# A vision tower on one core: the feed-forward's output columns in three pieces of nearly equal width

## The chip, the core and the metric

One of the eight cores of a Trainium2 chip runs the whole program. The core has TensorE (PE, with its weight loads shown as PEld), VectorE (DVE), ScalarE (ACT), GpSimd (POOL) and SyncE (SP, which here only issues DMAs). The metric is the device time of one execution in microseconds, median of several runs.

## What is computed

The input has 64 x 128 positions of states; the output has 64 rows of 129 tokens of 1024 channels. Three stages follow each other: a state-space kernel that turns each position into 1024 channels, a bidirectional state-space block behind a layer norm (down to 128 channels, two rounds, up again, with a residual), and a feed-forward part behind another layer norm, with a residual. The change touches the feed-forward part alone:

```python
def _L0_ffn_ref(x, base_W, base_b, router_W, router_b, A, B, expert_map):
    SCALING = 32.0 / 16.0
    E = A.shape[0]                                                        # 8 experts of rank 16
    base_out = jnp.einsum('btd,od->bto', x, base_W) + base_b              # 1024 -> 1024
    logits = jnp.einsum('btd,nd->btn', x, router_W) + router_b            # 1024 -> 15
    probs = jax.nn.softmax(logits, axis=-1)
    topk_p, topk_i = jax.lax.top_k(probs, E)
    mapped = expert_map[topk_i]
    onehot = (mapped[..., None] == jnp.arange(E)).astype(x.dtype)
    w = jnp.einsum('btk,btke->bte', topk_p, onehot)
    h = jnp.einsum('btd,erd->bter', x, A)                                 # 1024 -> 8 * 16 = 128
    lora = jnp.einsum('bter,eor->bto', h * w[..., None], B) * SCALING     # 128 -> 1024
    return base_out + lora
...
h = h + _L0_ffn_ref(_layernorm(h, axis=-1), ...)
```

## The kernel before

The work is cut into 65 tiles of 128 tokens (64 pairs of rows and one tile for the class token). It is pipelined by hand over iterations: in iteration i the first stage works on tile i, the state-space block on tiles i-1 and i-2, the up-projection and the second layer norm on tile i-4 (td in the code) and the feed-forward part on tile i-5 (te). Each engine has a `body` in which its steps stand in a fixed order, written out by hand; nothing but these lists and semaphores sets the order. `Step` holds one semaphore for each kind of step; `per` says how many increments a tile makes, and `wait(eng, n, name=j)` waits until tile n has made j of them. Iterations 8 to 61 run in a hardware loop of two iterations a turn, the others are written out.

On TensorE a tile's feed-forward is one product with a contraction of 1024 (eight slices k of 128) against the columns of `w_hi` and `w_lo`: 1024 columns of base_W, 128 of lora_A, 15 of the router and one of zeros. Each slice takes three matmuls (`ffn`, L1545: high part by high weights, high by low weights, low by high weights). The columns go to three banks of PSUM: `bases(0, ..)` and `bases(1, ..)` write 512 columns each to bank 0 and bank 1, and `route(a, b)` writes the 144 columns of lora_A and the router to bank 2. The pieces of `bases` and `route` stand between the steps of the other stages in the list at the end of TensorE's body: all of `route` and half of `bases` between `turn_x` and `project_out`, the rest of `bases` between `project_out` and `lora`. A matmul of 128 x 512 with `row_sel` (L1563) adds the bias at the start of each base half.

VectorE reads the router's logits out of bank 2 (`router(0)`, L1330), ScalarE takes the exponential, VectorE goes on (`router(1)` to `router(8)`), and `router(8)` (L1352) writes HW, the 128 lora columns weighted by expert. TensorE turns HW (`turn_h`, L1569, into bank 2), ScalarE and VectorE split it into HWS (`keep_w`, `weighted_lo` L1313), and TensorE adds the lora product to banks 0 and 1 (`lora(0)`, `lora(1)`, L1575 to L1577, 512 columns each). VectorE then adds both banks to the residual in HB (`final(0)`, `final(1)`, L1452), and SyncE stores HB.

Names of other steps that the next parts speak of: `project_out` (L1749) ends the state-space block's product, `layer_out` (L1319) copies it to U, `gated_b` (L1393) makes GT; `project_bc` (L1669) and `up` (L1587 to L1590) on TensorE wait for GT or its split GTS; `residual(h)` (L1401) adds the up-projection's halves to HB; `stats_2` (L1408) is the second layer norm's statistics, `shift_2` (L1421) its mean, `split_lo` (L1428) the low part of the normalized tile.

## Time and profile before

| | |
|---|---|
| median of 3 runs | 2318.59 us (2317.51 to 2318.93) |
| span of the profiled execution | 2315.8 us |
| TensorE busy | 2160.1 us, 93% of the span, 14117 matmul instructions |
| VectorE busy | 1843.7 us, 80% |
| ScalarE busy | 1527.5 us, 66% |
| GpSimd busy | 1095.6 us, 47% |
| `ffn` matmuls (L1545), 512 columns | 3 x 1040 instructions |
| `ffn` matmuls (L1545), 144 columns | 3 x 520 instructions |

The profiled execution is one run; its span goes from the first to the last instruction. The first 250 us prepare weights, then the iterations run. Matmuls are pipelined: one begins before the last has ended, so the busy time of a matmul (its duration) is longer than its distance to the next start, and a busy TensorE is not one at its peak.

### The profile page before, as it was taken

How to read it: one execution, taken by the hardware profiler on the slowest of the kernel's cores; microseconds unless marked ns; L12 is line 12 of the kernel's file. 1: busy time of each engine (PE TensorE's matmuls, PEld its weight loads, DVE VectorE, ACT ScalarE, POOL GpSimd, SP SyncE). 2: the span in 40 equal slices, each digit the busy share in tenths (PEclk: the TensorE clock that was granted, in tenths of full speed). 3: DMA queues.
4: the chain of work that ended last, by engine and by line, in shares of the span. 5: the costliest groups of instructions: out<-in, count | busy, mean ns of one | idle time of the engine just before them, and what ended most of it. 6: DMA issues, size and time to landing. Idle time of an engine off the chain costs nothing.

```text
span 2315.8 us, 51899 instructions
## 1 busy us (share of the span) xinstructions
PE 2160.1 (93%) x14117; PEld 1805.7 (78%) x14117; DVE 1843.7 (80%) x4980; ACT 1527.5 (66%) x2921; POOL 1095.6 (47%) x1350
## 2 busy tenths in 40 slices
PE   2366999999999999999999999999999999999997
PEld 2245888888888888888888888888888888888776
DVE  8666788888888888888888888888888888887763
ACT  4465676667766677666777667676676766767552
POOL 5543554445544455444554445544455444554321
PEclk8577999999999999999999999999999999999999
DMA  5201111222112221122221222212222112221111
GB/s 150 65 26 36 56 51 47 64 64 64 50 46 64 64 64 58 37 64 64 64 61 35 64 64 64 63 34 61 64 64 64 35 60 64 64 64 38 62 40 34
DMA packets 90061, 132.61 MB, mean 57 GB/s; under 512 B 20379, under 2 KB 63559, under 8 KB 90006
## 3 DMA queue, kind: packets, MB, share of 16 engines
q1 hardware_dynamic: 87496, 126.12, 18.4%
q10 hardware_dynamic: 2510, 5.83, 0.8%
q8 instruction: 25, 0.41, 0.1%
q14 instruction: 30, 0.25, 0.0%
HBM read 55.17 MB, written 76.74 MB: 57 GB/s over the span
## 4 chain that ended last, share of the span: by engine, by line
issue 44%; PE 27%; POOL 9%; DVE 7%; ACT 6%; POOLq 1%; DVEq 0%; ACTq 0%
PE bank L1644 5%; PE bank L1545 5%; POOL CB L934 4%; PE bank L1600 3%; PE bank L1575 2%; DVE NF L1274 2%; ACT L1039 2%; POOL XD L885 2%; PE bank L1718 2%; PE bank L1702 2%; POOL RS L919 1%; PE bank L1577 1%; PE bank L1576 1%; POOL RS L898 1%; PE bank L1692 1%
## 5 line engine op out<-in xcount | busy, mean ns | idle before, releaser
L1545 PE MATMUL bank<-w_hi,XHI 128*128 128x512 f32 (+1 forms) x1560 | 623.0, 399 | 0.0
L1545 PE MATMUL bank<-w_lo,XHI 128*128 128x512 f32 (+1 forms) x1560 | 555.1, 356 | 0.0
L1545 PE MATMUL bank<-w_hi,XLO 128*128 128x512 f32 (+1 forms) x1560 | 554.6, 355 | 0.0
L1180 DVE SCALAR_TENSOR_TENSOR CX<-bank,cw,CX 128x252 f32<-128x252 f32 (+5 forms) x804 | 335.6, 459 | 62.2 <-ACT CX L977 62.0
L934 POOL TENSOR_TENSOR CB<-CB,CM 48x252 f32<-48x252 f32 (+5 forms) x402 | 293.1, 729 | 153.5 <-ACT CM L962 142.6
L1545 PEld LDWEIGHTS bank<-w_hi,XLO 128*128 128x128 f32 x1560 | 295.5, 189 | 46.9
L1545 PEld LDWEIGHTS bank<-w_lo,XHI 128*128 128x128 f32 x1560 | 297.0, 190 | 41.2
L1545 PEld LDWEIGHTS bank<-w_hi,XHI 128*128 128x128 f32 x1560 | 296.7, 190 | 41.2
L962 ACT ACTIVATE T<-bank 64x512 f32<-64x512 f32 x256 | 151.4, 591 | 261.9 <-PE bank L1634 257.2
L898 POOL TENSOR_TENSOR RS<-VE,half_neg 128x1 f32<-128x1 f32 x65 | 35.5, 546 | 370.7 <-DVE VE L1372 370.7
L925 POOL TENSOR_TENSOR RB<-m_gt,AS 128x512 fp32r<-128x512 f32 x134 | 165.0, 1231 | 56.9 <-DVE AS L1446 56.9
L962 ACT ACTIVATE CM<-CR,cwb 48x256 f32<-48x256 f32 x402 | 181.4, 497 | 3.7 <-POOL CB L934 1.5
L892 POOL TENSOR_TENSOR RS<-MS,half_neg 128x2 f32<-128x2 f32 x67 | 46.9, 700 | 244.2 <-DVE MS L1303 244.2
L1634 PE MATMUL bank<-VB,W 128*128 128x256 f32 x512 | 149.4, 416 | 7.8 <-DVE W L1245 5.8
L1428 DVE TENSOR_TENSOR XLO<-bank,XHI 128x512 fp32r<-128x512 f32 x130 | 89.9, 692 | 73.1 <-ACT XHI L962 73.1
L1434 DVE TENSOR_TENSOR RF<-m_lt,AS 128x512 fp32r<-128x512 f32 x134 | 142.8, 1104 | 0.0
L962 ACT ACTIVATE XHI<-bank 128x512 fp32r<-128x512 f32 x130 | 77.6, 597 | 95.3 <-PE bank L1600 95.3
L1644 PE MATMUL bank<-XHT,wdT 128*128 128x128 f32 x1040 | 135.4, 286 | 4.5 <-ACT XHT L962 4.5
L1644 PEld LDWEIGHTS bank<-XHT,wdT 128*128 128x128 f32 x1040 | 129.2, 202 | 6.1 <-ACT XHT L962 6.1
L877 POOL TENSOR_TENSOR NB<-GB,sp_dt 128x512 f32<-128x512 f32 x67 | 96.0, 1433 | 77.5 <-DVE GB L1257 77.5
L885 POOL TENSOR_TENSOR XD<-XS,DD 128x512 f32<-128x512 f32 x67 | 84.7, 1264 | 98.5 <-DVE DD L1265 53.2
L1292 DVE TENSOR_TENSOR XD<-bank,XD 128x512 f32<-128x512 f32 x67 | 46.4, 692 | 79.1 <-POOL XD L885 58.2
(295 smaller groups left out, 5375.1 us busy)
## 6 DMA issues: line engine op xcount, KB each, us to landing
carried<-T SPq DMA_DIRECT2D x65, 512.0 KB, 4.7
T<-carried SPq DMA_DIRECT2D x65, 512.0 KB, 3.8
out<-HB SPq DMA_DIRECT2D x129, 256.0 KB, 3.2
tables<-tab SPq DMA_DIRECT2D x8, 560.0 KB, 4.1
TB<-tables SPq DMA_DIRECT2D x64, 70.0 KB, 2.7
carried<-U SPq DMA_DIRECT2D x65, 64.0 KB, 3.5
XM<-carried SPq DMA_DIRECT2D x65, 64.0 KB, 4.7
XI<-in_x SPq DMA_DIRECT2D x128, 32.0 KB, 2.7
```

Source lines behind the costliest of these rows:

```text
L877: inc(pool.tensor_tensor(NB[:, :, :].rearrange("p (a h) t -> p a h t", a=2), GB[:, :, :].unsqueeze(2).broadcast_to([P, 2, NH, CS]), dtB, A ...
L885: inc(pool.tensor_tensor(XD[:, :, :], v3(XS[:, :], HD), DD[:, :].unsqueeze(2).broadcast_to([P, 2 * NH, HD]), ALU.mult), "xd")
L925: inc(pool.tensor_tensor(RB[:, part, :, :], m_gt[:, :].unsqueeze(1).broadcast_to([P, 2 * NH, CS]), decays(1, part), ALU.mult), "rb")
L934: inc(pool.tensor_tensor(CB[:, :, s:CS], CB[:, :, s:CS], CM[:, s % 3, :, 0:CS - s], ALU.add), "cbc")
L962: inc(act.activation(dst, src, ACT.Copy, scale=scale), name)
L1180: inc(STT(CX[:, c, :, s:CS], src[:, :, 0:CS - s], cw[:, c, k:k + 1], CX[:, c, :, s:CS], ALU.mult, ALU.add), "conv")
L1428: inc(TT(XLO[:, p, ks, :], v3(bT[:, :], P), XHI[:, p, ks, :].bitcast(F32), ALU.subtract), "xlo")
L1434: inc(TT(RF[:, part, :, :], m_lt[:, :].unsqueeze(1).broadcast_to([P, 2 * NH, CS]), decays(0, part), ALU.mult), "rf")
L1545: ins = mm(bank[:, 0:c1 - c0], xs_[:, 1 - p, k, :], ws[:, k, c0:c1], start=(c0 == HID and k == 0 and n == 0), stop=(last == k and n == 2))
L1600: ins = tr(bT[:, P * k:P * (k + 1)], T2[:, (4 * g + k) * P:(4 * g + k + 1) * P], ident[:, :])
L1634: ins = mm(bK[:, 256 * s:256 * (s + 1)], W[:, b, 2 * s:2 * s + 2, :].rearrange("p a c -> p (a c)"), VB[:, b, :, :].rearrange("p a c -> p ( ...
L1644: ins = mm(bK[:, 0:P], wdT[:, k, :], XHT[:, k, :], start=(k == 0), stop=(k == KC - 1))
```

## The change

The 1024 base columns are cut at 384 and 768. `bases(0)` and `bases(1)` take 384 columns each into banks 0 and 1. `route` takes the remaining 256 base columns together with the 144 of lora_A and the router, 400 columns, into bank 2; their bias comes as an extra matmul of 256 columns behind the first one. Since bank 2 now holds base columns, the lora product of the last 256 columns is a product of its own in columns 256 to 511 of bank 2 (written over lora_A's and the router's columns, which have been read by then), and VectorE adds both: `final_first` adds the base part to HB right after `router(8)`, and the first `final` adds the lora part. HW is turned into a free part of bank 6 (`bY`) instead of bank 2. The increments per tile of `o` go from 2 to 3, those of `fin` from 2 to 4.

```diff
+    PIECES = ((0, 384), (384, 768), (768, 1024))
+    LA, LR = 256, 384
...
+        LORA = (2, 0, 1)
...
-                   rt=1, sm=NSM, se=1, hw=1, trh=1, hwe=1, hwl=1, o=2, fin=2)
+                   rt=1, sm=NSM, se=1, hw=1, trh=1, hwe=1, hwl=1, o=3, fin=4)
...
-                    wait(sp, t, fin=2)
+                    wait(sp, t, fin=4)
...
-                            copy(HWS[:, 0, :], bR[:, 256:384], "hwe", scale=2.0)
+                            copy(HWS[:, 0, :], bY[:, 384:512], "hwe", scale=2.0)
...
-                    def final(h):
+                    def final(n):
                         if E:
-                            wait(dve, te, o=h + 1)
-                            c = slice(HALF * h, HALF * (h + 1))
-                            inc(TT(HB[:, 1 - p, c], bO[h][:, :], HB[:, 1 - p, c], ALU.add), "fin")
+                            wait(dve, te, o=n + 1)
+                            c0, c1 = PIECES[LORA[n]]
+                            part = bR[:, LA:512] if LORA[n] == 2 else bO[LORA[n]][:, 0:c1 - c0]
+                            inc(TT(HB[:, 1 - p, c0:c1], part, HB[:, 1 - p, c0:c1], ALU.add), "fin")
+
+                    def final_first():
+
+                        if E:
+                            wait(dve, te, rt=1)
+                            c0, c1 = PIECES[2]
+                            inc(TT(HB[:, 1 - p, c0:c1], bR[:, 0:LA], HB[:, 1 - p, c0:c1], ALU.add), "fin")
...
                     router(8)
+                    final_first()
                     softplus(9)
...
                     final(0)
                     final(1)
+                    final(2)
...
                         for k in ks:
                             for n, (xs_, ws) in enumerate(((XHI, w_hi), (XHI, w_lo), (XLO, w_hi))):
                                 ins = mm(bank[:, 0:c1 - c0], xs_[:, 1 - p, k, :], ws[:, k, c0:c1],
-                                         start=(c0 == HID and k == 0 and n == 0), stop=(last == k and n == 2))
+                                         start=(start and k == 0 and n == 0), stop=(last == k and n == 2))
+                                if start and k == 0 and n == 0:
+                                    mm(bank[:, 0:LA], row_sel[:, :], base_bias[:, c0:c0 + LA], start=False, stop=False)
...
-                                wait(pe, te - 1, hwl=1)
-                            ins = ffn(HID, FW, bR, range(a, b), last=KC - 1)
+                                wait(pe, te - 1, fin=LORA.index(2) + 2)
+                            ins = ffn(PIECES[2][0], FW, bR, range(a, b), True, last=KC - 1)
...
-                                wait(pe, te - 1, fin=h + 1)
-                                mm(bO[h][:, :], row_sel[:, :], base_bias[:, HALF * h:HALF * (h + 1)], start=True, stop=False)
-                            ffn(HALF * h, HALF * (h + 1), bO[h], range(a, b))
+                                wait(pe, te - 1, fin=LORA.index(h) + 2)
+                                mm(bO[h][:, 0:c1 - c0], row_sel[:, :], base_bias[:, c0:c1], start=True, stop=False)
+                            ffn(c0, c1, bO[h], range(a, b), False)
...
-                            inc(tr(bR[:, 256:256 + P], HW[:, :], ident[:, :]), "trh")
+                            inc(tr(bY[:, 384:512], HW[:, :], ident[:, :]), "trh")
...
-                    def lora(h):
+                    def lora(n):
                         if E:
                             wait(pe, te, hwl=1)
-                            c = slice(HALF * h, HALF * (h + 1))
-                            mm(bO[h][:, :], HWS[:, 0, :], lb_hi[:, c], start=False, stop=False)
-                            mm(bO[h][:, :], HWS[:, 1, :], lb_hi[:, c], start=False, stop=False)
-                            inc(mm(bO[h][:, :], HWS[:, 0, :], lb_lo[:, c], start=False, stop=True), "o")
+                            c0, c1 = PIECES[LORA[n]]
+                            bank = bR[:, LA:512] if LORA[n] == 2 else bO[LORA[n]][:, 0:c1 - c0]
+                            mm(bank, HWS[:, 0, :], lb_hi[:, c0:c1], start=(LORA[n] == 2), stop=False)
+                            mm(bank, HWS[:, 1, :], lb_hi[:, c0:c1], start=False, stop=False)
+                            inc(mm(bank, HWS[:, 0, :], lb_lo[:, c0:c1], start=False, stop=True), "o")
...
                     lora(0)
                     lora(1)
+                    lora(2)
```

Line numbers of the kernel after are 13 lower on VectorE up to `split_decays`, since an empty head of the file went. On TensorE, at the start of a tile's feed-forward, before (bank 0 and bank 1 hold base columns, bank 2 lora_A and router):

```order
L1563 MATMUL bank0<-base_bias,row_sel 128x512
L1545 MATMUL bank0<-w_hi,XHI 128x512
L1545 MATMUL bank0<-w_lo,XHI 128x512
L1545 MATMUL bank0<-w_hi,XLO 128x512
L1545 MATMUL bank2<-w_hi,XHI 128x144
L1545 MATMUL bank2<-w_lo,XHI 128x144
L1545 MATMUL bank2<-w_hi,XLO 128x144
L1563 MATMUL bank1<-base_bias,row_sel 128x512
```

and after:

```order
L1563 MATMUL bank0<-base_bias,row_sel 128x384
L1542 MATMUL bank0<-w_hi,XHI 128x384
L1542 MATMUL bank0<-w_lo,XHI 128x384
L1542 MATMUL bank0<-w_hi,XLO 128x384
L1542 MATMUL bank2<-w_hi,XHI 128x400
L1545 MATMUL bank2<-base_bias,row_sel 128x256
L1542 MATMUL bank2<-w_lo,XHI 128x400
L1542 MATMUL bank2<-w_hi,XLO 128x400
L1563 MATMUL bank1<-base_bias,row_sel 128x384
```

The places of the pieces are the same; 128 columns of each base half have gone to the pieces of `route`, and one bias matmul is new. On TensorE at the end of the tile's feed-forward, where the lora product waits for HWS, before:

```order
L1545 MATMUL bank1<-w_hi,XLO 128x512
L1575 MATMUL bank0<-lb_hi,HWS 128x512
L1576 MATMUL bank0<-lb_hi,HWS 128x512
L1577 MATMUL bank0<-lb_lo,HWS 128x512
L1575 MATMUL bank1<-lb_hi,HWS 128x512
L1576 MATMUL bank1<-lb_hi,HWS 128x512
L1577 MATMUL bank1<-lb_lo,HWS 128x512
L1600 MATMUL bank4<-ident,T2 128x128 x4
```

and after:

```order
L1542 MATMUL bank1<-w_hi,XLO 128x384
L1576 MATMUL bank2<-lb_hi,HWS 128x256
L1577 MATMUL bank2<-lb_hi,HWS 128x256
L1578 MATMUL bank2<-lb_lo,HWS 128x256
L1576 MATMUL bank0<-lb_hi,HWS 128x384
L1577 MATMUL bank0<-lb_hi,HWS 128x384
L1578 MATMUL bank0<-lb_lo,HWS 128x384
L1576 MATMUL bank1<-lb_hi,HWS 128x384
L1577 MATMUL bank1<-lb_hi,HWS 128x384
L1578 MATMUL bank1<-lb_lo,HWS 128x384
L1601 MATMUL bank4<-ident,T2 128x128 x4
```

Two groups of three became three, the one for bank 2 first. On VectorE, between HW (`router(8)`) and HWS, on which the lora product waits, before (sp_p, sp_dt and sp_aa are steps of a softplus, VE and NM belong to the second layer norm, CX is the convolution):

```order
L1352 SCALAR_TENSOR_TENSOR HW<-bank,RE,WE 128x128
L1210 SCALAR_TENSOR_TENSOR sp_p<-sp_p,sp_w 128x16
L1212 SCALAR_TENSOR_TENSOR sp_p<-sp_p,sp_z 128x16
L1215 SCALAR_TENSOR_TENSOR sp_dt<-sp_x,sp_p 128x16
L1415 TENSOR_SCALAR VE<-MV 128x1
L1180 SCALAR_TENSOR_TENSOR CX<-bank,cw,CX 128x4x58
L1217 TENSOR_TENSOR sp_aa<-sp_dt,negA 128x16
L1421 SCALAR_TENSOR_TENSOR NM<-MV,RS 128x1
L1180 SCALAR_TENSOR_TENSOR CX<-bank,cw,CX 128x4x58
L1443 CAST AS<-sp_aa 128x16
L1313 SCALAR_TENSOR_TENSOR HWS<-bank,HWS 128x128
```

and after:

```order
L1339 SCALAR_TENSOR_TENSOR HW<-bank,RE,WE 128x128
L1447 TENSOR_TENSOR HB<-bank,HB 128x256
L1197 SCALAR_TENSOR_TENSOR sp_p<-sp_p,sp_w 128x16
L1199 SCALAR_TENSOR_TENSOR sp_p<-sp_p,sp_z 128x16
L1202 SCALAR_TENSOR_TENSOR sp_dt<-sp_x,sp_p 128x16
L1402 TENSOR_SCALAR VE<-MV 128x1
L1167 SCALAR_TENSOR_TENSOR CX<-bank,cw,CX 128x4x58
L1204 TENSOR_TENSOR sp_aa<-sp_dt,negA 128x16
L1408 SCALAR_TENSOR_TENSOR NM<-MV,RS 128x1
L1167 SCALAR_TENSOR_TENSOR CX<-bank,cw,CX 128x4x58
L1430 CAST AS<-sp_aa 128x16
L1300 SCALAR_TENSOR_TENSOR HWS<-bank,HWS 128x128
```

The new sum of 256 columns (L1447) stands between HW and the rest; the others keep their order.

## Rows read from the trace of the kernel before

**Rows 1.** Stretch, length; busy PE, PEld, DVE, ACT, POOL (instructions); PEclk; DMA share; GB/s.

```profile
600.00:2200.00 1600.00, 1586.75 (x10587) 1333.41 (x10585) 1315.41 (x3635) 1110.26 (x2136) 778.85 (x938) 1.00 0.19 58
```

**Rows 2.** Who waited for L1313, the line that completes HWS: us, times.

```profile
  PEld bank L1575: 34.4, 63
```

**Rows 3.** Busy time in one stretch of a tile, columns as in rows 1.

```profile
1225.08:1235.76 10.68, 10.51 (x51) 7.79 (x49) 10.04 (x43) 8.58 (x18) 4.55 (x8) 1.00 0.00 0
```

**Rows 4.** TensorE in order of time, one tile: start, duration, line, matmul.

```profile
1203.83 0.50 PE L1575 MATMUL bank<-lb_hi,HWS 128*128 128x512 f32 x1
...
1223.92 1.02 PE L1749 MATMUL bank<-NF,owT 128*128 128x256 f32 x4
...
1225.25 0.39 PE L1545 MATMUL bank<-w_hi,XLO 128*128 128x512 f32 x1
1225.78 0.58 PE L1669 MATMUL bank<-wbc,U 128*128 128x8 f32 x4
...
1229.99 0.39 PE L1590 MATMUL bank<-wu_lo,GTS 128*128 128x512 f32 x1
...
1235.33 0.40 PE L1545 MATMUL bank<-w_hi,XLO 128*128 128x512 f32 x1
1235.81 0.50 PE L1575 MATMUL bank<-lb_hi,HWS 128*128 128x512 f32 x1
```

**Rows 5.** VectorE in order of time, the same tile.

```profile
1224.81 0.15 DVE L1333 TENSOR_REDUCE NM<-LG 128x1 f32<-128x15 f32 x1
1225.08 0.29 DVE L1319 COPY U<-bank 128x128 f32<-128x128 f32 x1
...
1228.23 0.69 DVE L1401 TENSOR_TENSOR HB<-bank,T 128x512 f32<-128x512 f32 x1
...
1229.71 0.68 DVE L1408 BATCH_NORM_STATS2 ST<-HB 128x6 f32<-128x512 f32 x1
1230.42 0.69 DVE L1401 TENSOR_TENSOR HB<-bank,T 128x512 f32<-128x512 f32 x1
...
1235.48 0.28 DVE L1313 SCALAR_TENSOR_TENSOR HWS<-bank,HWS 128x128 fp32r<-128x128 f32 x1
```

**Rows 6.** TensorE in order of time: runs of equal matmuls, first and after last.

```profile
1209.98 0.39 PE L1718 MATMUL bank<-RB,later 128*128 128x256 f32 x2
...
1210.66 0.27 PE L1652 MATMUL bank<-ident,XI 128*128 128x128 f32 x1
...
1212.39 0.40 PE L1545 MATMUL bank<-w_hi,XHI 128*128 128x512 f32 x1
...
1213.79 0.23 PE L1545 MATMUL bank<-w_hi,XHI 128*128 128x144 f32 x1
...
1214.90 0.28 PE L1545 MATMUL bank<-w_lo,XHI 128*128 128x144 f32 x1
...
1215.35 0.27 PE L1545 MATMUL bank<-w_hi,XLO 128*128 128x144 f32 x1
```

**Rows 7.** TensorE in order of time near the end; in brackets idle time and releaser.

```profile
2293.72 0.51 PE L1563 MATMUL bank<-base_bias,row_sel 128*128 128x512 f32 x1 [1.41 <-DVE XLO L1428]
...
2296.07 0.63 PE L1545 MATMUL bank<-w_hi,XHI 128*128 128x512 f32 x1
...
2296.93 0.63 PE L1545 MATMUL bank<-w_hi,XLO 128*128 128x512 f32 x1
```

**Rows 8.** VectorE in order of time: last sums of a tile, then products from PSUM.

```profile
1207.30 1.28 DVE L1452 TENSOR_TENSOR HB<-bank,HB 128x512 f32<-128x512 f32 x2
...
1210.29 0.28 DVE L1254 TENSOR_TENSOR GF<-bank,m_lt 128x126 f32<-128x126 f32 x1
1210.49 0.28 DVE L1257 TENSOR_TENSOR GB<-bank,m_gt 128x126 f32<-128x126 f32 x1
```

**Rows 9.** Busy time and PE clock in two stretches near the end, columns as in rows 1.

```profile
2295.00:2297.50 2.50, 2.50 (x9) 2.11 (x8) 0.00 (x0) 0.00 (x0) 0.00 (x0) 0.50 0.42 128
2302.00:2309.60 7.60, 7.60 (x35) 6.08 (x33) 1.96 (x9) 0.59 (x3) 0.00 (x0) 1.00 0.00 0
```

More of the change, by code:

```diff
@@ L698, in build @@
         HW = sb("HW", [P, P])
-        bO = banks[0:2]
+        bO = banks[0:3]
         bR = banks[2]
+        LORA = (2, 0, 1)
         bK = banks[3]
@@ L1072, in keep_w @@
                             wait(act, te, trh=1)
-                            wait(act, te - 1, o=2)
-                            copy(HWS[:, 0, :], bR[:, 256:384], "hwe", scale=2.0)
+                            wait(act, te - 1, o=3)
+                            copy(HWS[:, 0, :], bY[:, 384:512], "hwe", scale=2.0)
                     def exp_dt():
@@ L1108, in split_hi @@
                             wait(act, td, tr2=g + 1)
-                            wait(act, td - 2, o=2)
+                            wait(act, td - 2, o=3)
                             copy(XHI[:, p, 4 * g:4 * g + 4, :], v3(bT[:, :], P), "xhi")
@@ L1312, in weighted_lo @@
                             wait(dve, te, hwe=1)
-                            inc(STT(HWS[:, 1, :], bR[:, 256:384], 2.0, HWS[:, 0, :].bitcast(F32), ALU.mult, ALU.subtract), "hwl")
+                            inc(STT(HWS[:, 1, :], bY[:, 384:512], 2.0, HWS[:, 0, :].bitcast(F32), ALU.mult, ALU.subtract), "hwl")
                     def layer_out():
@@ L1329, in router @@
                             wait(dve, te - 1, se=1)
-                            inc(TT(LG[:, :], bR[:, P:P + NR], rbias[:, :], ALU.add), "sm")
+                            inc(TT(LG[:, :], bR[:, LR:LR + NR], rbias[:, :], ALU.add), "sm")
                         elif j == 1:
@@ L1351, in router @@
                             wait(dve, te - 1, trh=1)
-                            inc(STT(HW[:, :].rearrange("p (e r) -> p e r", e=NE), bR[:, 0:P].rearrange("p (e r) -> p e r", e=NE),
+                            inc(STT(HW[:, :].rearrange("p (e r) -> p e r", e=NE), bR[:, LA:LR].rearrange("p (e r) -> p e r", e=NE),
                                     RE[:, 0:1], WE[:, :].unsqueeze(2).broadcast_to([P, NE, RK]), ALU.mult, ALU.mult), "hw")
@@ L1425, in split_lo @@
                             wait(dve, td, xhi=g + 1)
-                            wait(dve, td - 2, o=2)
+                            wait(dve, td - 2, o=3)
                             ks = slice(4 * g, 4 * g + 4)
@@ L1539, in body, with ffn @@
                     u = U[:, 1 - p, :, :].rearrange("p a t -> p (a t)")
-                    def ffn(c0, c1, bank, ks, last=None):
+                    def ffn(c0, c1, bank, ks, start, last=None):
                         for k in ks:
@@ L1559, in bases @@
                         if E:
+                            c0, c1 = PIECES[h]
                             if a == 0:
                                 wait(pe, te, xlo=2)
-                                wait(pe, te - 1, fin=h + 1)
-                                mm(bO[h][:, :], row_sel[:, :], base_bias[:, HALF * h:HALF * (h + 1)], start=True, stop=False)
-                            ffn(HALF * h, HALF * (h + 1), bO[h], range(a, b))
+                                wait(pe, te - 1, fin=LORA.index(h) + 2)
+                                mm(bO[h][:, 0:c1 - c0], row_sel[:, :], base_bias[:, c0:c1], start=True, stop=False)
+                            ffn(c0, c1, bO[h], range(a, b), False)
                     def turn_h():
```

## The prediction

> **What bounds the kernel now.** I read the busy time of a long stretch first, then who waits at the lora product, then one tile's turn in time order on TensorE and on VectorE, and last the distances between starts of equal matmuls. From 600 to 2200 us TensorE is busy 1586.75 of 1600 us at clock 1.00 and VectorE 1315.41 [rows 1]. By that view alone a shorter TensorE stream would shorten everything. The second view says otherwise. HWS, the weighted expert activations that VectorE writes before the lora product, is made once for each of 65 tiles, and TensorE's first lora weight load waited for it 63 times, 34.4 us in all [rows 2]. So at that place of every tile TensorE is early and VectorE is late.
>
> The timelines close this into a loop. The first lora matmul starts at 1203.83 and the next tile's at 1235.81: 31.98 us a tile [rows 4]. In between, project_out's matmuls start at 1223.92 and end at 1224.94, and VectorE's copy U, which needs them, starts at 1225.08, although VectorE was done with its last reduction at 1224.96 [rows 4, 5]. From U VectorE works through to HWS, done at 1235.76 after 10.04 busy of 10.68 us [rows 3], and lora starts 0.05 later [rows 4, 5]. TensorE's 10.51 there are durations that overlap its waits. A turn is therefore two stretches end to end: **the TensorE stretch**, lora to U, 21.25 us, in which TensorE sets the time, and **the VectorE stretch**, U to the next lora, 10.73 us, in which TensorE waits: 0.3 us before project_bc (a 512-column step from 1225.25 ends at 1225.48, the next matmul starts at 1225.78) and 0.25 before lora (1235.33 plus 0.23 against 1235.81) [rows 4]. What matters is in which stretch a matmul stands, not how many are saved.
>
> **Step prices.** A matmul's price is the distance to the next start. 512 columns: six between 1212.39 and 1213.79, 0.233 us each. 144 columns: four between 1214.90 and 1215.35, 0.1125 each. 256 columns of the same number type: six between 1209.98 and 1210.66, 0.113 each [rows 6]. 384 and 400 columns do not occur; they lie between 0.113 and 0.233. I take the straight line between 256 and 512: **0.173 and 0.181**. For a lower end, at half clock two 512-column steps take 2296.07 to 2296.93, 0.43 each [rows 7], so the columns alone would take 0.215 at full clock, and the measured step is 0.018 over that. Columns alone give 0.161 for 384 and 0.168 for 400. At 256 columns the excess is 0.006 (0.113 against 0.107), so it grows faster than the columns, which is why the line should not be far too low. An upper end carries the whole 0.018 over to both: 0.179 and 0.186.
>
> **The change, TensorE.** Per tile 48 matmuls go from 512 to 384 columns (-0.060 each) and 24 from 144 to 400 (+0.068). Together that is -1.2 us, but it is not spread evenly.
> - TensorE stretch (lora to project_out): lora goes from 6 x 0.233 = 1.40 to 3 x 0.113 + 6 x 0.173 = 1.38, -0.02. Bias goes from 2 x 0.233 to 2 x 0.173 plus one of 0.113, -0.01. All 24 matmuls with lora_A and the router stand here: +1.64. Only 24 of the base ones do (eight pieces of three): -1.44. Sum **+0.18 us**. This stretch gets longer, since all the columns that moved landed in it.
> - VectorE's own work ahead of U, which hangs on an earlier product of the same stretch (s4d), was done at 1224.96 for a start of U at 1225.08 [rows 5]. Up to s4d 12 base matmuls and 12 of 400 columns stand: -0.72 + 0.82, with lora and bias +0.07. So that work moves by less than project_out does, and U goes on waiting for project_out.
> - VectorE stretch: the other 24 base matmuls, -1.44 us. TensorE already waits twice here. It will wait about 1.7 us longer, in front of lora and of the turn of HW. I count 0 for this.
> - The places inside the TensorE stretch where another engine might be late stay covered: the turn of HW now writes a free part of the bank of the projections, lora waits for the same HWS, and the new waits on fin are on the sums of the tile before, which end at 1208.58 [rows 8], while the base matmuls only follow the 256-column steps that begin at 1209.98 [rows 6].
>
> **The change, VectorE.** A new sum of 256 columns (final_first) stands between HW and the rest of softplus, inside the VectorE stretch. Two 512-column sums take 1.28 together [rows 8] and one such sum lasts 0.69 [rows 5], so a step is 0.59; the step of a 126-column product out of a bank is 0.20 [rows 8]. The line between gives 0.33 for 256 columns (ends 0.20 and 0.59): **+0.33 us**, queued ahead of softplus, stats_2, shift_2 and HWS, so lora waits for it. Nothing in this stretch hides it, because VectorE is busy 10.04 of 10.68 us here [rows 3], and what it lacks to 10.68 are waits that move along with it.
> One gap closes. The second residual sum starts at 1230.42, just after up's last matmul (1229.99 plus 0.39), while VectorE's bn_stats ended at 1230.39 [rows 4, 5]; sums that wait for nothing overlap their forerunner by 0.1 (0.69 against the step of 0.59), so back to back it would start up to 0.13 sooner. The two base pieces ahead of up(1) shrink by 0.36, and up(1) only needs the first residual sum (1228.23 plus 0.69), so it runs earlier: **-0.1 us** (ends -0.13 and 0).
> The last sums become 256, 384 and 384 columns instead of 512 and 512, some 0.07 longer. They stand behind split_lo(0), where VectorE next waits for ACT; 0, and 0.07 if that cover is gone. The output's DMA leaves with the fourth sum, as much later, and its buffer is next written most of a tile later: 0.
>
> Sum per tile: 0.18 + 0.33 - 0.1 = **+0.41 us**. Tiles pass the feed-forward in 65 iterations, 59 of them with all other stages running: +24.2. In the last iteration TensorE runs the FFN nearly alone (busy 7.60 of 7.60 us, VectorE 1.96 [rows 9]), so the full 1.2 comes off, and with the iteration before I give back 2. Sum **+22.2 us**. The profiled span is 2315.8, 2.8 under the median of the runs, 2318.6; I add to the median: **2341 us**, 1.0% slower.
>
> **What the Trainium skill would say.** The trace has 0.233 us for 512 columns at full clock [rows 6]. The Trainium skill, TensorE: Matmul & The Clock Gate, section Back-to-back issue gap, gives columns over 2.4 GHz plus 2.5 ns for an isolated matmul: 0.216 for 512, 0.1625 for 384, 0.169 for 400. The trace disagrees at 512 by 0.017. By that rule the TensorE stretch would shorten, and the total would come out faster by about as much as rival two below, which is reckoned from rows.
>
> **The rivals.**
> 1. TensorE is the bound after all, and the wait at lora only an exposed weight load. Then 65 x 1.2 = 78 us come off: 2240. For it: 99% busy. Against it: 63 waits that name HWS [rows 2], and HWS ending 0.05 before lora starts [rows 4, 5]. Chance 0.05.
> 2. Faster: 384 and 400 columns cost their columns alone, 0.161 and 0.168. In the TensorE stretch 24 + 24 + 2 + 6 = 56 such matmuls are each 0.0125 cheaper than I take, -0.70, so a tile is 0.29 shorter: 59 x -0.29 - 2 = -19, **2299**. It decides from a 384 step under about 0.166, where the 0.41 are used up. For it: the half-clock rows. Against it: the 512 step misses that rate by 0.018. Chance 0.07; and 0.09 for steps near 0.166, no change.
> 3. Slower still: the 0.018 is per matmul, and up(1) gives nothing back: 56 x 0.0055 + 0.1 = +0.41, so 0.82 a tile, 48 - 2 = +46: **2365**. It is my own case with its upper ends.
> 4. The clock falls, since TensorE now waits some 1.7 us more a tile. The one late stretch at half clock (0.50, the 1.2 GHz level) from 2295 on follows waits of TensorE, the last of 1.41 us, and a 512 step takes 0.43 there [rows 7, 9]; if 3 us of each tile ran so, 1.5 us a tile or +90 come on top: 2430. Against it: the waits here are shorter and stand between matmuls, and the clock is 1.00 through 1600 us with waits already there [rows 1]. Chance 0.03.
> 5. The change does not do what it says: a step costs the same whatever its columns. The 144 rows at 0.1125 speak against it; 24 x 0.12 more a tile would be over 2500. Chance 0.01.
>
> **How the numbers follow.** My forecast with its bounds, rival 3 included, has 0.75. Faster by over 0.2% (the least that a measurement of this kernel can tell from no change): rivals 1 and 2, 0.12. Within 0.2%: 0.09. Slower: 0.75 + 0.03 + 0.01 = 0.79. The range goes from half way into rival 2, 2309, to just over rival 3, 2367; left out are rivals 1, 4, 5 and the far part of 2.
>
> **What would show it.** Right: 384-column steps near 0.173 and 400 near 0.181; lora to lora near 32.4 us; U starting about 0.18 later after lora; final_first at a step of 0.33 between HW and softplus; the wait at lora grown from 0.25 to over 1 us; the page's TensorE share falling by several per cent while the span grows. Wrong: a wait at lora that stays small, so that TensorE sets the pace through both stretches, or 384 steps at 0.166 or less.

## The result, and the profile after

The changed kernel takes 2361.43 us (median of four runs, 2358.88 to 2364.33), the kernel before 2318.76. The ratio is 1.0185, 95% interval 1.0171 to 1.0200: slower by 42.7 us, where the forecast was +22 with a range up to 2367. The profiled spans, 2357.1 and 2315.8, differ by 41.3. All times and ratios here are of runs in the usual state of the clock; one run of four of b2_narrow_early, below, took 3363 us at a granted clock of 0.55 and is left out.

The long stretch of rows 1, in the kernel after, columns as there:

```profile
600.00:2200.00 1600.00, 1524.67 (x10599) 1374.23 (x10597) 1308.72 (x3657) 1090.51 (x2097) 765.09 (x924) 1.00 0.19 57
```

In these 1600 us TensorE went from 1586.75 busy microseconds to 1524.67: it has less to do and the kernel is slower. The clock in this stretch is 1.00 as before. Where TensorE waits now is read from its waits. Three lines of the kernel after (weight load, line, what released it: us in total, times, longest):

```profile
PEld bank L1576 <- DVE HWS L1300: 88.1, 64, 3.2
...
PEld bank L1569 <- DVE HW L1339: 36.0, 64, 1.3
...
PEld bank L1588 <- DVE HB L1388: 14.5, 56, 1.2
```

and the last two of them in the kernel before (the first is rows 2, 34.4):

```profile
PEld bank L1569 <- DVE HW L1352: 2.2, 4, 0.6
...
PEld bank L1587 <- DVE HB L1401: 1.5, 1, 1.5
```

All three places (lora, the turn of HW, up) lie between U and lora, and each is a wait for VectorE. Counted at the weight loads they grew by 100.5 us together, while the kernel grew by 42.7.

One tile of the kernel after on TensorE, in order of time (the tile of rows 4 and 6):

```profile
1219.58 0.39 PE L1576 MATMUL bank<-lb_hi,HWS 128*128 128x256 f32 x1 [1.03 <-DVE HWS L1300]
...
1226.56 0.42 PE L1563 MATMUL bank<-base_bias,row_sel 128*128 128x384 f32 x1
...
1228.19 0.34 PE L1542 MATMUL bank<-w_hi,XHI 128*128 128x384 f32 x1
...
1229.24 0.34 PE L1542 MATMUL bank<-w_hi,XHI 128*128 128x400 f32 x1
...
1230.32 0.35 PE L1542 MATMUL bank<-w_hi,XHI 128*128 128x400 f32 x1
...
1231.23 0.34 PE L1542 MATMUL bank<-w_hi,XLO 128*128 128x400 f32 x1
1231.50 1.15 PE L1731 MATMUL bank<-XS,Mt 64*64 64x64 f32 x32
1232.58 1.13 PE L1635 MATMUL bank<-VB,W 128*128 128x256 f32 x4
...
1240.02 1.02 PE L1750 MATMUL bank<-NF,owT 128*128 128x256 f32 x4
...
1252.23 0.39 PE L1576 MATMUL bank<-lb_hi,HWS 128*128 128x256 f32 x1 [1.03 <-DVE HWS L1300]
```

The same marks in the kernel before that rows 4 and 6 don't have:

```profile
1210.80 0.48 PE L1563 MATMUL bank<-base_bias,row_sel 128*128 128x512 f32 x1
...
1215.55 1.15 PE L1730 MATMUL bank<-XS,Mt 64*64 64x64 f32 x32
1216.63 1.13 PE L1634 MATMUL bank<-VB,W 128*128 128x256 f32 x4
```

Lora to lora is 32.65 us, 0.67 more than the 31.98 of rows 4. From lora to the first bias matmul it is 6.98 (before 6.97), from there to mix 4.94 (before 4.75), mix to s4d 1.08 in both, s4d to project_out 7.44 (before 7.29). So the two places with base pieces and matmuls of 400 columns carry +0.19 and +0.15. Six 384-column steps take 1228.19 to 1229.24, 0.175 each, and five of 400 take 1230.32 to 1231.23, 0.182 each.

VectorE in the same tile, after (answers to rows 5):

```profile
1240.76 0.15 DVE L1320 TENSOR_REDUCE NM<-LG 128x1 f32<-128x15 f32 x1
1241.18 0.29 DVE L1306 COPY U<-bank 128x128 f32<-128x128 f32 x1 [0.28 <-PE bank L1750]
...
1246.40 0.68 DVE L1388 TENSOR_TENSOR HB<-bank,T 128x512 f32<-128x512 f32 x1
...
1247.72 0.29 DVE L1193 TENSOR_TENSOR sp_w<-sp_z 128x16 f32<-128x16 f32 x1
1248.05 0.17 DVE L1195 TENSOR_SCALAR sp_p<-sp_w 128x16 f32<-128x16 f32 x1
...
1248.98 0.35 DVE L1339 SCALAR_TENSOR_TENSOR HW<-bank,RE,WE 128x128 f32<-128x128 f32 x1
1249.25 0.42 DVE L1447 TENSOR_TENSOR HB<-bank,HB 128x256 f32<-128x256 f32 x1
1249.58 0.17 DVE L1197 SCALAR_TENSOR_TENSOR sp_p<-sp_p,sp_w 128x16 f32<-128x16 f32 x1
...
1251.90 0.28 DVE L1300 SCALAR_TENSOR_TENSOR HWS<-bank,HWS 128x128 fp32r<-128x128 f32 x1
```

and before:

```profile
1231.75 0.16 DVE L1206 TENSOR_TENSOR sp_w<-sp_z 128x16 f32<-128x16 f32 x1
1231.95 0.18 DVE L1208 TENSOR_SCALAR sp_p<-sp_w 128x16 f32<-128x16 f32 x1
...
1232.89 0.35 DVE L1352 SCALAR_TENSOR_TENSOR HW<-bank,RE,WE 128x128 f32<-128x128 f32 x1
```

Three things stand there. U still starts 1.16 behind project_out, as in rows 4 and 5, and VectorE was done at 1240.91, so it waited for project_out. The new sum (L1447) takes a step of 1249.25 to 1249.58, 0.33, and HW to HWS goes from 2.59 to 2.92. And the second residual sum starts 5.22 after U instead of 5.34, so its gap closed by 0.12, but one small step further on, sp_p stands 6.87 after U in both kernels: sp_w took 0.29 instead of 0.16 and ate it. GpSimd's sum of shifted projections beside it, after and before:

```profile
1247.28 0.70 POOL L921 TENSOR_TENSOR CB<-CB,CM 48x240 f32<-48x240 f32 x1 [0.52 <-ACT CM L949]
```

```profile
1231.19 0.69 POOL L934 TENSOR_TENSOR CB<-CB,CM 48x240 f32<-48x240 f32 x1 [0.52 <-ACT CM L962]
```

It ends at 1247.98 and 1231.88, and sp_w ends at 1248.01 and 1231.91, 0.03 behind it in both. sp_w now starts earlier within that sum, and ends with it all the same.

So 0.67 is +0.35 from lora to U and +0.32 from U to lora. Not every tile grew as much, and the end of the run grew by more. From the first lora to the 57th, with which the hardware loop ends, the kernel after loses 35.5 us, 0.63 a tile. It reaches the first one 2.5 us sooner, and needs 8.3 us more from the 57th to the end, at a lower granted clock (columns as in rows 1; before, after, and the 58th lora after):

```profile
2070.00:2315.80 245.80, 225.84 (x1442) 185.34 (x1442) 161.05 (x463) 127.02 (x252) 84.24 (x97) 0.98 0.17 48
```

```profile
2103.00:2357.10 254.10, 225.32 (x1477) 202.31 (x1477) 162.69 (x480) 127.24 (x252) 84.39 (x97) 0.96 0.16 47
```

```profile
2137.34 0.41 PE L1576 MATMUL bank<-lb_hi,HWS 128*128 128x256 f32 x1 [2.85 <-DVE HWS L1300]
```

Behind this wait of 2.85 us the 384-column steps of lora are 0.32 us (2138.30 to 2138.62) instead of 0.175: the clock is at its lower level, 1.2 GHz. The three tiles that start at 2137.34, 2267.00 and 2301.20 have a granted clock of 0.95, 0.90 and 0.89, where the same three in the kernel before have 1.00, and they took 7.6 us longer together. The tile ahead of the first of them took 2.5 longer, since VectorE stood still for 2.52 us ahead of HWS; the profile shows no reason for that. The very last tile took 2.5 us less.

### The profile page after: what moved, and what is told of

Its sections match the earlier page's. It is cut to its first block, busy times and chain, and to the rows that moved or that the text cites. A ratio compares the mean times of both kernels' runs of the same rounds, so it can differ in the third digit from the quotient of the medians.

```text
span 2357.1 us, 52684 instructions
## 1 busy us (share of the span) xinstructions
PE 2115.1 (90%) x14377; PEld 1892.1 (80%) x14377; DVE 1868.0 (79%) x5110; ACT 1528.3 (65%) x2921; POOL 1094.3 (46%) x1350
## 4 chain that ended last, share of the span: by engine, by line
issue 45%; PE 25%; POOL 10%; DVE 8%; ACT 6%; POOLq 1%; DVEq 1%; ACTq 0%
PE bank L1645 5%; POOL CB L921 4%; PE bank L1542 4%; PE bank L1601 3%; PE bank L1576 2%; DVE NF L1261 2%; ACT L1026 2%; PE bank L1719 2%; PE bank L1703 2%; POOL XD L872 1%; POOL RS L906 1%; DVE CX L1167 1%; PE bank L1577 1%; PE bank L1578 1%; POOL RS L885 1%
## 5 line engine op out<-in xcount | busy, mean ns | idle before, releaser
L1542 PE MATMUL bank<-w_hi,XHI 128*128 128x384 f32 (+1 forms) x1560 | 610.0, 391 | 0.0
L1542 PE MATMUL bank<-w_lo,XHI 128*128 128x384 f32 (+1 forms) x1560 | 530.3, 340 | 0.0
L1542 PE MATMUL bank<-w_hi,XLO 128*128 128x384 f32 (+1 forms) x1560 | 529.7, 340 | 0.0
L1542 PEld LDWEIGHTS bank<-w_lo,XHI 128*128 128x128 f32 x1560 | 295.1, 189 | 10.9
L885 POOL TENSOR_TENSOR RS<-VE,half_neg 128x1 f32<-128x1 f32 x65 | 35.5, 546 | 376.4 <-DVE VE L1359 376.4
L1635 PE MATMUL bank<-VB,W 128*128 128x256 f32 x512 | 144.1, 405 | 7.7 <-DVE W L1232 5.8
L1576 PE MATMUL bank<-lb_hi,HWS 128*128 128x384 f32 (+1 forms) x195 | 70.2, 360 | 67.9 <-DVE HWS L1300 67.9
```

The lines of the kernel that those rows point to most:

```text
L1542: ins = mm(bank[:, 0:c1 - c0], xs_[:, 1 - p, k, :], ws[:, k, c0:c1], start=(start and k == 0 and n == 0), stop=(last == k and n == 2))
L1576: mm(bank, HWS[:, 0, :], lb_hi[:, c0:c1], start=(LORA[n] == 2), stop=False)
L1635: ins = mm(bK[:, 256 * s:256 * (s + 1)], W[:, b, 2 * s:2 * s + 2, :].rearrange("p a c -> p (a c)"), VB[:, b, :, :].rearrange("p a c -> p ( ...
```

## Experiments

Stretches in us, each the mean of the 41 to 48 tiles between 600 and 2120 us, read from the timelines; a few odd tiles among them move a mean by some 0.05 against the tile shown above. All ratios are to the kernel before, run on the same chip; it took 2317 to 2320 us there, so two times of the table can be compared to a few us only.

| kernel | lora to U | U to HW | HW to lora | tile | time | ratio (95%) |
|---|---|---|---|---|---|---|
| before | 21.39 | 7.78 | 2.93 | 32.09 | 2318.76 | |
| after | 21.69 | 7.77 | 3.29 | 32.76 | 2361.43 | 1.0185 (1.0171 to 1.0200) |
| b1_narrow_late | 21.39 | 7.77 | 2.93 | 32.09 | 2316.88 | 0.9993 (0.9981 to 1.0006) |
| b2_narrow_early | 20.89 | 7.78 | 2.92 | 31.59 | 2283.46 | 0.9844 (0.9809 to 0.9879) |
| b3_before_two_pieces | 20.77 | 7.78 | 4.06 | 32.61 | 2347.68 | 1.0129 (1.0112 to 1.0146) |
| e1_sum_late | 26.83 | 7.78 | 2.93 | 37.53 | 2645.88 | 1.1405 (1.1385 to 1.1425) |
| e8_sum_late_rb_waits | 21.69 | 7.77 | 2.96 | 32.42 | 2339.65 | 1.0104 (1.0087 to 1.0121) |
| e5_sum_after_decays | 21.76 | 7.77 | 2.96 | 32.49 | 2338.14 | 1.0075 (1.0049 to 1.0102) |
| e2_piece_moved | 21.54 | 7.77 | 3.29 | 32.60 | 2348.74 | 1.0130 (1.0113 to 1.0146) |
| e4_conv_before_softplus | 21.69 | 7.74 | 3.28 | 32.71 | 2361.14 | 1.0189 (1.0172 to 1.0206) |
| e7_short_add_beside | 21.69 | 7.64 | 3.28 | 32.61 | 2350.76 | 1.0141 (1.0124 to 1.0158) |
| e6_sum_and_two_pieces | 21.08 | 7.77 | 2.96 | 31.80 | 2293.77 | 0.9883 (0.9857 to 0.9908) |

### In which stretch a matmul counts: b1, b2

The kernel before, with 24 of the 48 base matmuls a tile narrowed to 384 columns: those behind project_out (b1) or those ahead of it (b2, with `not in`). Both leave out the products with the columns that are cut off.

```
-ffn(HALF * h, HALF * (h + 1), bO[h], range(a, b))
+ffn(HALF * h, HALF * h + (384 if (h, a) in ((0, 5), (1, 3), (0, 6), (1, 4), (0, 7), (1, 5), (1, 6), (1, 7)) else HALF), bO[h], range(a, b))
```

> The kernel before, with the eight base pieces that stand between project_out and lora narrowed from 512 to 384 columns (24 matmuls a tile); their products with 128 columns of the base weights are left out. Theory (in that stretch TensorE waits for VectorE): no change, 2318, with TensorE's waits at lora and at the turn of HW 1.4 us longer a tile; up to -6 if the second residual sum starts 0.1 sooner. Rival (TensorE's work sets the time wherever it stands): 62 x -1.4 = -87, 2231.

> The kernel before, with the eight base pieces that stand between lora and project_out narrowed from 512 to 384 columns (24 matmuls a tile); their products with 128 columns of the base weights are left out. Theory (in that stretch TensorE sets the time, until VectorE's own work ahead of U is late): the pieces ahead of the s4d matmuls give their full 0.7 us, those behind about 0.15; 0.85 a tile or -53: 2265. Upper end, if nothing else is late: -1.4 a tile, 2231. Rival (VectorE is late everywhere, TensorE's columns count nowhere): 2318.

b1 left out 24 x 0.058 = 1.4 us of TensorE work a tile and changed nothing that can be told; at the weight loads the waits grew by 78 us, 1.2 a tile:

```profile
PEld bank L1575 <- DVE HWS L1313: 65.5, 63, 1.4
...
PEld bank L1569 <- DVE HW L1352: 36.3, 64, 1.3
...
PEld bank L1587 <- DVE HB L1401: 14.5, 55, 1.5
```

The last two are those of the kernel after, and the first lacks 22.6 us of it, about what the new sum in front of HWS adds there (64 times 0.33). b2 left out the same work ahead of U and gained 36 us. That settles rival 1 and the loop of two stretches. But b2 gained 0.50 a tile of the 0.85 that I expected, as another wait came up behind it:

```profile
PEld bank L1749 <- ACT NF L962: 30.6, 62, 1.4
...
PEld bank L1634 <- issue: 22.8, 56, 3.7
```

The first names ScalarE's input to project_out, for which it waited 5.3 us in 8 tiles before; the second is a wait at s4d whose releaser the profile doesn't show. So the stretch from lora to U has a second limit some 0.5 us behind TensorE.

### What the sum costs, and what it can collide with: e1, e8, e5

e1 moves the sum from between HW and HWS to just ahead of decays_forth (RF), and lora's third piece to the end, where it waits for the sum, since it shares the bank.

```
-                    final_first()
                     softplus(9)
...
                     split_decays(1)
+                    final_first()
                     decays_forth(0)
...
-        LORA = (2, 0, 1)
+        LORA = (0, 1, 2)
```

> The changed kernel with its new sum final_first moved out of VectorE's stretch from U to HWS: it now follows split_decays(1), behind HWS, and bank 2's lora product comes last of the three and waits for it. Theory of the two stretches: U to HWS gets 0.33 to 0.37 us shorter, lora to U stays, a tile takes 32.40 instead of 32.76 us, 59 x 0.36 = 21 us come off: 2340. Rival, the longer TensorE stream or its new waits make the whole loss: no change, 2361.

HW to lora came back by the 0.36, and lora to U grew by 5.1 us. Both theories missed it. VectorE and GpSimd of e1 in order of time:

```profile
1215.72 0.41 DVE L1447 TENSOR_TENSOR HB<-bank,HB 128x256 f32<-128x256 f32 x1
1216.05 5.86 DVE L1421 TENSOR_TENSOR RF<-m_lt,AS 128x512 fp32r<-128x512 f32 x2
```

```profile
1215.87 1.04 POOL L912 TENSOR_TENSOR RB<-m_gt,AS 128x512 fp32r<-128x512 f32 x1 [0.82 <-DVE AS L1433]
1216.88 1.04 POOL L921 TENSOR_TENSOR CB<-CB,CM 48x232 f32<-48x232 f32 x1
1217.88 1.04 POOL L912 TENSOR_TENSOR RB<-m_gt,AS 128x512 fp32r<-128x512 f32 x1
1218.91 1.19 POOL L900 TENSOR_SCALAR T<-T,SD,NM 128x1024 f32<-128x1024 f32 x1
1220.05 0.28 POOL L833 COPY XSW<-XI 128x128 f32<-128x128 f32 x1
1220.31 1.05 POOL L840 TENSOR_TENSOR V<-TB 128x512 f32<-128x512 f32 x1
```

and, in the kernel after:

```profile
1252.18 2.13 DVE L1421 TENSOR_TENSOR RF<-m_lt,AS 128x512 fp32r<-128x512 f32 x2
```

```profile
1252.34 1.43 POOL L912 TENSOR_TENSOR RB<-m_gt,AS 128x512 fp32r<-128x512 f32 x1 [0.82 <-DVE AS L1433]
```

The two RF products, 2.13 us in the kernels before and after, take 5.86 here, and end at 1221.91, 0.55 behind the end of GpSimd's unbroken row of instructions at 1221.36. In the kernels before and after RF starts 0.16 ahead of RB. Here the sum has put RF 0.33 later, and RB starts first. What follows RF is late, TensorE's turn of T above all (all tiles, then the tile shown, then the long stretch of e1):

```profile
PEld bank L1603 <- DVE XLO L1415: 189.0, 64, 3.1
```

```profile
1222.57 0.66 PE L1603 MATMUL bank<-ident,T 128*128 128x128 f32 x4 [2.89 <-DVE XLO L1415]
```

```profile
600.00:2200.00 1600.00, 1424.24 (x9229) 1285.39 (x9227) 1279.77 (x3211) 955.78 (x1836) 627.37 (x813) 0.94 0.16 48
```

In this tile lora to s4d takes 17.71 us, 4.71 more than in the tile of the kernel after. This turn of T, the second, starts 6.80 us behind lora, which is 3.07 of them. Some 1.6 more are the clock: from the turn to the first 400-column matmul e1 needs 5.61 us and the kernel after 4.04, and 384-column steps are 0.32 us there (1227.22 to 1227.54), the lower level again. Over the long stretch the granted clock is 0.94 in e1 and 0.91 in e3; in all other runs it is 1.00.

e8 is e1 with one line more: GpSimd's RB waits for the RF of the same half.

```
                             wait(pool, q, asp=2)
+                            wait(pool, q, rf=part + 1)
```

> The run e1 (final_first ahead of decays_forth, lora's third piece last), with one addition: GpSimd's products RB wait for VectorE's products RF of the same half, so that RF comes first again. Theory (e1 lost 5 us a tile only because RB started first and RF then stood still until GpSimd's row of instructions was through): RF back to 1.1 us mean, lora to s4d back from 18.2 to 13.1 or at most 13.9 us (RB is later by up to 1), so 2340 to 2390. Rival (what cost e1 its 5 us is the sum's place itself, or the wait of lora's third piece): RF stays near 3 us or lora to s4d near 18.2, about 2646.

Lora to s4d came back from 18.23 to 13.09 us, the RF products to 0.68 on average (2.78 in e1), and the time to 2339.65. The order of RF and RB was the cause of e1, not the sum's place. The clock is 1.00 again. The price is that GpSimd waits 96.8 us for RF in the whole run, which costs no time that can be seen beside e5 below.

e5 puts the sum behind both RF, and lora's third piece behind down, where TensorE otherwise goes on to turn_d(1).

> The 256-column sum final_first is taken out of the softplus steps and put behind both calls of decays_forth (the products RF), with the lora piece that needs it moved behind the down projection. So VectorE no longer does it between HW and HWS, and RF starts as early behind HWS as in the changed kernel. Theory (final_first costs its own 0.33 to 0.36 us a tile only because lora waits for HWS behind it, and the run with the sum ahead of RF was long only because RF then met GpSimd's product RB): 62 tiles x -0.36 = -22 us against the changed kernel's 2361, that is 2339; the stretch from HW to HWS back from 2.96 to 2.60 us; RF at 1.10 us mean. Rival A (VectorE's place between HW and HWS does not set the time): 2361. Rival B (the reordered sums themselves, by banks or waits, were what made that run long): again near 2640, with RF near 3 us.

2338.14, with HW to lora back by 0.33. e5 and e8 agree on what the sum costs where the change has it: 0.33 in this stretch of each tile. The whole tile is 0.27 and 0.34 shorter than in the kernel after, since lora to U is 0.07 longer in e5. Over 56 tiles that is 15 and 19 us of the 22 to 23 that they are faster; the rest lies at the ends of the run.

### Where the residual sum's gain went: e4, e7

e4 swaps conv(5, 1) ahead of softplus(5), so that sp_w starts after GpSimd's sum has ended.

```
+                    conv(5, 1)
                     softplus(5)
                     softplus(6)
-                    conv(5, 1)
```

> The changed kernel with the convolution step conv(5, 1) moved ahead of softplus(5) and softplus(6) on VectorE. In the changed kernel softplus(5) takes 0.29 us against 0.17 before, and ends just after a GpSimd add that runs beside it. Theory, it waits for that add: behind the convolution it starts after the add and takes 0.17, a tile 32.64, 59 x 0.12 = 7 off: 2354. Rival, softplus(5) is slow for a cause of its own (bn_stats just ahead): still 0.29 wherever it stands or no time gained, 2361.

No change that can be told: 0.04 a tile. sp_w fell to 0.176 on average, but the small steps that hang on it now follow each other with nothing between. So sp_w is short once the sum has ended, and whether its length costs time stayed open. e7 shortens GpSimd's sum instead, and leaves out 176 of its 240 columns:

```
-inc(pool.tensor_tensor(CB[:, :, s:CS], CB[:, :, s:CS], CM[:, s % 3, :, 0:CS - s], ALU.add), "cbc")
+e = s + 16 if s == 4 else CS
+inc(pool.tensor_tensor(CB[:, :, s:e], CB[:, :, s:e], CM[:, s % 3, :, 0:e - s], ALU.add), "cbc")
```

> The changed kernel, with one of GpSimd's five sums of shifted projections per tile (the one of 240 columns, which runs beside VectorE's softplus step sp_w) cut to 64 columns; the other 176 columns are left out of the sum. Theory (sp_w, 0.29 us in the changed kernel and 0.17 in the one before, is long only because it starts while that sum runs and ends with it, and this eats the 0.1 us that the second residual sum gave back): sp_w again 0.16 to 0.17, HWS 0.1 sooner, 62 x -0.1 = -6, 2355. It may give less, since the small steps behind it hang on each other. Rival (sp_w is longer for reasons of its own, such as the order of the steps ahead of it): sp_w stays at 0.29, 2361.

The durations of sp_w (ns: least, median, most) in the kernel after and in e7:

```profile
L1193 DVE TENSOR_TENSOR sp_w<-sp_z x67: 150/291/302, 132.1 to 2297.0; 128x16 f32<-128x16 f32 x67
```

```profile
L1194 DVE TENSOR_TENSOR sp_w<-sp_z x67: 149/157/175, 132.5 to 2290.7; 128x16 f32<-128x16 f32 x67
```

From U to HW 0.13 us went, a tile is 0.14 shorter, and the kernel some 10 us faster. So sp_w was long because of the sum beside it, and it held back the 0.1 that I had counted. That GpSimd's operation ends sp_w's delay is shown; how the two engines hinder each other inside is not. The Trainium skill, SBUF — State Buffer, section SBUF: two separate sides, says that VectorE and GpSimd share a pair of ports that is locked for a whole instruction, for VectorE operations with two SBUF inputs against a GpSimd one that reads SBUF; the 0.03 to 0.04 us from GpSimd's end to sp_w's in every tile of both kernels between 600 and 2120 us, and e7, agree with it.

### Work moved to where TensorE waits: e2, b3, e3, e6

e2 is the changed kernel with one base piece (three matmuls) moved from ahead of turn_y to ahead of lora, where TensorE waits.

```
-                    bases(0, 2, 3)
                     bases(0, 3, 4)
...
+                    bases(0, 2, 3)
                     lora(0)
```

> The changed kernel with one base piece of three 384-column matmuls (bases(0, 2, 3)) moved from before turn_y to just before lora: the same work on TensorE, another stretch. Theory: 0.53 us leave the stretch lora to U, of which some 0.3 are gained until VectorE's own work ahead of U binds; the wait at lora takes the piece in. A tile 32.45, 59 x 0.3 = 18 off: 2343. Rival, the sum of TensorE's work counts: no change, 2361.

Lora to U gave 0.15 of the piece's 0.52, where I expected 0.3: project_out came 0.25 sooner, and then U started 1.27 behind it instead of 1.17, since VectorE's own work ahead of U was late (U waited for project_out 7 times instead of 60). e3 adds e1's place of the sum and a second piece, bases(0, 1, 2), moved from ahead of mix to ahead of turn_h.

> The changed kernel with the sum late as in the first kernel of this set, the piece of the second moved, and one more piece (bases(0, 1, 2), ahead of the mixing step) moved to before the turn of HW. Theory: 0.36 from U to HWS, 0.53 before s4d, 0.3 between s4d and U: a tile 31.57, 59 x 1.19 = 70 off: 2291, below the kernel before. If TensorE becomes late at lora with two pieces more in that stretch, up to 0.3 of it is lost: 2309. Rival, only the sum counts: 2340.

2646.58, ratio 1.1419 (1.1400 to 1.1438): it has e1's collision and tells nothing of the moves. e6 is e5 with these two moves, and b3 the kernel before with them.

> As the run with the sum behind the decays, and two base pieces (six matmuls of 384 columns, 1.05 us) taken out of the stretch from lora to U and put into the stretch in which TensorE waits: one ahead of the turn of HW, one ahead of lora. Theory (two stretches end to end; matmuls count only in the first): the piece that stood ahead of the s4d matmuls takes 0.52 off lora to s4d, the one behind them only 0.15, since VectorE's own work ahead of U then comes last; with -0.36 for the sum, 1.03 a tile or -64 us against 2361: 2297, faster than the kernel before. Rival A (TensorE's busy time is the bound, wherever a matmul stands): as the run with the sum alone, about 2339 or 2361. Rival B (VectorE's chain ahead of U is late at once when s4d comes sooner): the 0.52 does not come, 2330.

> The kernel before, with the same two base pieces moved as in the run with the sum and two pieces: six matmuls of 512 columns, 1.4 us, out of the stretch from lora to U, one piece ahead of the turn of HW and one ahead of lora. Theory (matmuls cost nothing behind U only as far as TensorE waits there, and in the kernel before it waits 0.25 us ahead of lora): lora to U shortens by about 0.5 us, and U to lora lengthens by up to 1.4 - 0.25 = 1.15, so +0.65 a tile or +40: 2358, slower; at best, if the turn of HW is not late, +0.1: 2325. Rival (the two moves alone are the gain, the narrower pieces are not needed): -0.5 a tile, 2287.

e6 takes 2293.77, 1.2% less than the kernel before: it beats both. Its lora to U is 0.68 shorter than e5's, and nothing was added behind U. In b3 the same two moves make the kernel before slower, with TensorE late at lora, 1.17 behind the end of HWS at 1253.26:

```profile
1254.43 0.40 PE L1575 MATMUL bank<-lb_hi,HWS 128*128 128x512 f32 x1
```

```profile
1252.98 0.28 DVE L1313 SCALAR_TENSOR_TENSOR HWS<-bank,HWS 128x128 fp32r<-128x128 f32 x1
```

So the moves alone don't do it. The narrower pieces make the room between U and lora (the waits of the kernel after), the moves use it, and e6's place of the sum gives back the rest. A smaller move in the kernel before, of a matmul or two into the 0.55 us that TensorE waits there, was not run. e6 still waits at lora, and at project_out for ScalarE as b2 does (29.7 us in 62 tiles):

```profile
PEld bank L1578 <- DVE HWS L1300: 28.3, 63, 1.7
```

## Why the prediction was right, and what it mis-sized

- **Two stretches, and only matmuls from lora to U count**: right. b1, b2 and b3 show it, and TensorE's wait behind U grew by 100.5 us over 64 tiles, 1.6 a tile, against the 1.7 forecast. Rival 1 falls.
- **TensorE stretch +0.18**: the sign was right, the term too small, +0.35 in the tile shown and in the median, +0.30 in the mean. The step that failed is the price of a step: the line between 256 and 512 columns gave 0.173 and 0.181, the trace has 0.175 and 0.182. Over 24 matmuls of 400 columns, 24 base ones, two for the bias and lora's six of 384 that is some 0.1. Of the other 0.07 some 0.02 is lora's three matmuls of 256 columns, which step at 0.12 and not 0.113. Some 0.04 comes from pricing every width by itself. Between the first bias matmul and mix, the kernel before takes only 0.06 to 0.07 us over a 144-column matmul that follows one of 512 (three times, 1213.79 to 1213.86 is one) instead of 0.1125, and 0.28 over one of 512 that follows one of 144 (twice, 1214.08 to 1214.36 is one) instead of 0.233; the kernel after has widths of 384 and 400 side by side. Rival 2 falls, since the steps are above the 0.166 under which it decides. By the Trainium skill, TensorE: Matmul & The Clock Gate, section Back-to-back issue gap, which gives columns over 2.4 GHz plus 2.5 ns for an isolated matmul, an estimate of the steps is 0.1625 and 0.169; the trace disagrees with it at both widths, by 0.013.
- **U goes on waiting for project_out**: right, 1.16 in both kernels. But the cover is thin: e2 shows it gone after 0.15.
- **final_first +0.33**: right to the hundredth, by its step in the trace and by e5 and e8. The table's +0.36 from HW to lora is 0.32 in the median; one odd tile at 2103 us makes the difference.
- **up(1) and the residual sum, -0.1**: wrong. The sum did start 0.12 sooner, but I named no work that would be late next. It was sp_w, held by GpSimd's sum, and e7 gives the 0.14 back when that sum is short.
- **The last sums at 0**: no run singled them out.
- **The clock** (rival 4): 1.00 in the long stretch, where the rival falls. Behind the loop it came true in part: three tiles lost 7.6 us with a lower clock, which the sum has at nothing. Nor was the stretch from 2295 us on the only late one at a lower clock: from 2196 to 2229 the kernel before has 0.95.
- **59 tiles and 2 us given back at the end**: the last tile did give back 2.5, but the seven ahead of it lost 10.9, the three with the lower clock among them.

A tile lost 0.63 us in the mean of the loop against the 0.41 forecast. Of the 20 us by which 42.7 exceeds 22.2, this makes some 12 over 56 tiles; the end of the run makes most of the rest. That the time still lies in the range is in part luck. Its upper end is rival 3, of which one half came true (up(1) gives nothing back) and the other didn't (steps of 0.179 and 0.186), and the room that this left took in the lower clock at the end, which neither sum has.

## What to carry to other kernels

A step that makes the busiest engine's work smaller pays only in the stretch in which that engine sets the time: cut the loop at its hand-overs, put each saved and each added operation in its stretch, and if the saving falls where the engine already waits, move other work into the wait (e6) before judging the change. Where a step starts sooner, look at the next operation on its engine that shares a resource with another engine's operation that has not moved. And keep the order in which two engines start on their large products: 0.33 us of delay cost 5 us a tile in e1, some 1.6 of them in the tile shown because TensorE's clock fell behind the long wait.

## What was not expected of the hardware

A VectorE product with two inputs in SBUF that starts behind a GpSimd one can be held through several GpSimd instructions on end: two RF products took 5.86 us instead of 2.13. The first got its turn behind RB: it took 1.41 us and ended 0.55 behind RB's end. The second took 4.53 and ended 0.55 behind the last of five GpSimd instructions. What decides whether VectorE gets a turn between two of them is open. An RF product that nothing holds takes 0.68 us (e8) and sp_w 0.157 (e7), and sp_w ended 0.03 to 0.04 behind the sum: all three end behind GpSimd's instruction by their own length less 0.12 to 0.13 us. And a step between equal matmuls is 0.175 us for 384 columns and 0.182 for 400, a little over the line between the 0.113 and 0.233 of rows 6, so a matmul of these widths costs about the same 0.455 ns a column as one of 512, and only 256 columns come cheaper, at 0.44.
